# Load order, early layer norms on GpSimd, and matrix squarings held by an identity factor in the setup stage of a two-layer kernel

## The reference

```python
# layer 0
h = layernorm(x) * (1 + ca) + sa                 # sa, ca, ga, ... = silu(c) @ wmod
p = h @ proj_w + proj_b                          # three parts of 128 columns
v = p[0]
for stage in range(2):                           # a convolution with 256 taps through a 512-point FFT
    v = irfft(rfft(v) * rfft(filter[stage])) * p[stage + 1]
x = x + ga * v
x = x + gb * (feed_forward(h) + product_key_experts(h))
# layer 1
x = x + ga * differential_attention(h)           # 16 heads, causal
moe = mixture_of_8_experts(h)                    # w1, gelu, w2, top 2
for i in range(3):
    moe = moe @ expm(gens[i])                    # three 128 x 128 rotations
x = x + gb * gated_mix(abel(h), moe)
```

## Time and profile before

| what | value |
|---|---|
| median of 3 runs | 1199.24 us |
| time of the profiled execution | 1201.76 us |
| span of its profile | 1200.5 us |
| granted TensorE clock, mean | 0.981 |
| busy: TensorE / weight load / VectorE / ScalarE / GpSimd | 1099.8 / 798.7 / 951.9 / 676.3 / 446.5 us |
| first and last transfer of the bulk load | issued at 0.72 us, traffic ends near 34.5 us |
| stage 2 begins (first L1220) | 161.03 us |

### The profile page before, as it was taken

One profiled execution on the slowest core, in us unless ns is written; L12 is line 12 of the kernel. 1 busy time (PEld: TensorE's weight loads), 2 busy tenths in 40 slices (PEclk: granted clock), 3 DMA queues, 4 the chain that ended last, 5 costly groups with the idle time before them and its releaser, 6 DMA issues.

```text
span 1200.5 us, 23140 instructions
## 1 busy us (share of the span) xinstructions
PE 1099.8 (92%) x7614; PEld 798.7 (67%) x7614; DVE 951.9 (79%) x3327; ACT 676.3 (56%) x1739; POOL 446.5 (37%) x724
## 2 busy tenths in 40 slices
PE   0876768999999899999999999999999999999997
PEld 0775734666666676777777677777767777656766
DVE  2496969899998769878888888888888888755767
ACT  0220124555555656776777777767777777744441
POOL 0416413123332315544444444444444555423310
PEclk9998979999999999999999999999999999999999
DMA  9100030000000000000000000000000000000000
GB/s 274 49 1 1 1 106 1 1 1 2 1 1 2 1 1 1 1 1 2 1 1 1 2 2 1 1 1 2 2 1 1 2 1 2 2 1 5 8 9 16
DMA packets 19956, 15.32 MB, mean 13 GB/s; under 512 B 2432, under 2 KB 18816, under 8 KB 19712
## 3 DMA queue, kind: packets, MB, share of 16 engines
q1 hardware_dynamic: 19840, 13.86, 3.9%
HBM read 12.81 MB, written 1.05 MB: 12 GB/s over the span
## 4 chain that ended last, share of the span: by engine, by line
PE 71%; DVE 16%; ACT 5%; issue 4%; POOL 3%; DMA 1%; SPq 1%; DVEq 0%; POOLq 0%; ACTq 0%
PE bank L1549 11%; PE bank L1579 10%; PE bank L1543 10%; PE bank L1498 7%; PE bank L986 5%; PE bank L1887 5%; PE bank L1908 4%; PE bank L1519 3%; PE bank L1527 3%; PE bank L971 2%; ACT prb L1614 2%; DVE prob L1304 2%; DVE xm_e L729 1%; PE bank L964 1%; PE bank L946 1%
## 5 line engine op out<-in xcount | busy, mean ns | idle before, releaser
L1645 POOL TENSOR_SCALAR prb<-prb,rnorm 128x512 f32<-128x512 f32 (+3 forms) x512 | 270.6, 545 | 348.1 <-DVE rnorm L1735 348.0
L1614 ACT ACTIVATE prb<-prb,negmax 128x512 f32<-128x512 f32 (+3 forms) x512 | 281.0, 552 | 113.4 <-DVE negmax L1717 113.4
L1717 DVE CUSTOM_DVE_ANT_0 prb<-bank,mask 128x512 f32<-128x512 f32 (+3 forms) x512 | 218.8, 483 | 18.5 <-PE bank L1543 18.3
L1549 PE MATMUL bank<-ident,prb 128*128 128x128 f32 x1280 | 158.4, 275 | 3.6 <-POOL prb L1645 3.1
L1549 PEld LDWEIGHTS bank<-ident,prb 128*128 128x128 f32 x1280 | 139.6, 141 | 23.3 <-issue 11.6
L1579 PE MATMUL bank<-prbT,vv 128*64 128x512 f32 (+3 forms) x1024 | 151.9, 439 | 0.0
L1579 PEld LDWEIGHTS bank<-prbT,vv 128*64 128x64 f32 x1024 | 63.4, 136 | 82.0 <-issue 81.9
L1622 ACT ACTIVATE prbT<-bank 128x512 f32<-128x512 f32 x128 | 76.5, 597 | 61.2 <-PE bank L1549 60.3
L1726 DVE COPY prbT<-bank 128x512 f32<-128x512 f32 x128 | 87.7, 690 | 14.8 <-PE bank L1549 14.4
L1614 ACT ACTIVATION_READ_ACCUMULATOR prb<-prb,negmax 128x1 f32 x512 | 97.0, 189 | 0.0
L1945 ACT ACTIVATE h<-bank,eb1T 128x512 f32<-128x512 f32 x64 | 43.7, 686 | 55.4 <-PE bank L1887 55.1
(11 more groups left out here) (450 smaller groups left out, 2397.5 us busy)
## 6 DMA issues: line engine op xcount, KB each, us to landing
x<-in_x SPq DMA_DIRECT2D x2, 512.0 KB, 5.9
ew2T<-in_ew2T SPq DMA_DIRECT2D x1, 1024.0 KB, 8.3
ew<-in_ew SPq DMA_DIRECT2D x1, 1024.0 KB, 5.8
wq<-in_Wq SPq DMA_DIRECT2D x2, 512.0 KB, 5.1
wk<-in_Wk SPq DMA_DIRECT2D x2, 512.0 KB, 7.4
wv<-in_Wv SPq DMA_DIRECT2D x1, 1024.0 KB, 8.1
out<-res SPq DMA_DIRECT2D x16, 64.0 KB, 1.5
wmod<-in_wmod SPq DMA_DIRECT2D x2, 384.0 KB, 5.9
```

Source lines behind the costliest of these rows:

```text
L1549: last = T.transpose(into[:, at + (qc - kc) * P:at + (qc - kc + 1) * P], prb[j % 2][:, i, p_at[qc] + kc * P:p_at[qc] + (kc + 1) * P], iden ...
L1614: A.activation(v, v, ACT.Exp, scale=-1.0, bias=negmax[j % 2][:, place[qc], i:i + 1], accum_out=rowsum[j % 2][:, place[qc], i:i + 1]).then_ ...
L1645: last = G.tensor_scalar(v, v, rnorm[j % 2][:, place[qc], i:i + 1], 1.0, ALU.mult, ALU.mult)
L1717: V.tensor_tensor_reduce(prb[j % 2][:, i, p_at[qc]:p_at[qc] + (qc + 1) * P], s_of(j, s, i, qc), mask[:, (NT - 1 - qc) * P:S], 1.0, LARGEST ...
```

## The change

The transfer of `x` for batches 0 and 1 is issued first and `cT`, `small`, `ident` behind it. `c_inv` goes ahead of `gens2` (`xm_b`), and `eb2T` moves behind `ew2T`. GpSimd no longer takes part in the rotations: the maximum over the columns comes from a TensorE transpose, a VectorE maximum and a TensorE broadcast product, and L646 is gone. A finished matrix is held another way: its side 1 is set to the identity, so that the next product leaves side 0 as it is. ScalarE copies side 0 (128x384) and prepares the diagonals keep*I; VectorE does only side 1 (three of 128x128). The rotations begin five rounds in, and the first squaring stands at round 17. The layer norms of batches 2 and 3 get places of their own for `xhat`, `mv` and `rstd` and are done in `setup_*` at round 10, so the second batches' convolutions take 25 rounds. VectorE's first modulation moves behind both first statistics.

```diff
+            SP.dma_start(x[:, 0:2, :, :], tokens[:, 0:2, :, :]).then_inc(x01_in, 16)
             for l in range(2):
                 SP.dma_start(cT[l][:, :], a[f"cT{l}"]).then_inc(first_in, 16)
...
+            SP.dma_start(c_inv[:, :, :], a["c_inv"]...).then_inc(inv_in, 16)
             SP.dma_start(xb, a["gens2"]...).then_inc(rot_in, 16)
-            SP.dma_start(eb2T[:, :], a["eb2T"]).then_inc(rot_in, 16)
...
+            yield from idle(OFFSET)
+            modulation_vector(0)
+            yield from idle(3 + 2 * ORDER + 1 - OFFSET)
             modulation_vector(1)
+            yield from idle(2)
+            V.wait_ge(x23_in, 16)
+            for k in range(2):
+                layernorm_vector(lanes[k], 1, x[:, 2 + k, :, :])
...
+        def rotations_scalar():
+            yield from idle(START + 12)
+            A.wait_ge(xm_ready, 5)
+            for k in range(MAX_SQUARINGS):
+                if k:
+                    A.wait_ge(xm_ps, 4 + k)
+                    A.activation(xe[:, :, 0, :], product(0), ACT.Copy).then_inc(xm_act, 1)
+                if k + 1 < MAX_SQUARINGS:
+                    for i in range(NROT):
+                        last = A.activation(diagonal(k + 1, i), ident[:, :], ACT.Identity, scale=keep[:, k + 1, i:i + 1])
+                    last.then_inc(xm_act, 1)
...
+            yield from idle(START + 1)            # rotations_tensor, START = 5
+            T.wait_ge(xm_norm, 1)
+            T.transpose(bank[0][0:NROT, 0:P], norm[:, :], ident[:, :]).then_inc(xm_all, 1)
+            yield
+            T.wait_ge(xm_norm, 2)
+            T.matmul(bank[0][:, P:P + NROT], largest[:, :].broadcast_to([NROT, P]), ident[0:NROT, 0:NROT], ...)
...
-            G.partition_all_reduce(normall[:, :], norm[:, :], P, MAX_REDUCE).then_inc(xm_all, 1)
-                G.tensor_tensor(kept[k % 2]..., xe..., keep[:, k, :]..., ALU.mult).then_inc(xm_old, 1)
...
+            for i in range(NROT):                 # before the first squaring
+                dve.did(V.tensor_scalar(xe[:, i, 1, :], xe[:, i, 1, :], over[:, 0, i:i + 1], None, ALU.mult))
+            dve.settle()
+            for i in range(NROT):
+                last = V.scalar_tensor_tensor(xe[:, i, 1, :], ident[:, :], keep[:, 0, i:i + 1], xe[:, i, 1, :], ALU.mult, ALU.add)
...
-                    last = V.scalar_tensor_tensor(xe[:, i, :, :], product(i), over[:, k, i:i + 1], old[:, i, :, :], ALU.mult, ALU.add)
+                V.wait_ge(xm_act, DIAGONAL_KEPT(k))
+                    last = V.scalar_tensor_tensor(xe[:, i, 1, :], product(1)[:, i, :], over[:, k, i:i + 1], diagonal(k, i), ALU.mult, ALU.add)
```

More of the change, by code:

```diff
@@ L15 @@
 AX = mybir.AxisListType
-MAX_REDUCE = bass.bass_isa.ReduceOp.max
 P = 128
@@ L424, in sync_program @@
             SP.wait_ge(stored, 16 * NT * B)
+        OFFSET = 2
         def modulation_tensor(l):
@@ L594, in products @@
                     for side in range(2):
-                        last = T.matmul(product(i)[:, side, :], left[:, i, 1 - side, :], right[:, i, side, :],
+                        last = T.matmul(product(side)[:, i, :], left[:, i, 1 - side, :], right[:, i, side, :],
                                         start=True, stop=True)
                 last.then_inc(xm_ps, 1)
-            yield from idle(4)
-            T.wait_ge(rot_in, ROT_IN)
+            yield from idle(START + 1)
+            T.wait_ge(xm_norm, 1)
+            T.transpose(bank[0][0:NROT, 0:P], norm[:, :], ident[:, :]).then_inc(xm_all, 1)
+            yield
+            T.wait_ge(xm_norm, 2)
+            T.matmul(bank[0][:, P:P + NROT], largest[:, :].broadcast_to([NROT, P]), ident[0:NROT, 0:NROT], start=True, stop=True).then_inc(xm_all, 1)
+            yield
+            yield
             products(xb, xb, 1)
@@ L637, in rotations_tensor @@
             yield
-        def rotations_gpsimd():
-            G.wait_ge(xm_norm, 1)
-            G.partition_all_reduce(normall[:, :], norm[:, :], P, MAX_REDUCE).then_inc(xm_all, 1)
[L642 to L650, removed]
         def rotations_vector():
-            V.wait_ge(rot_in, ROT_IN)
+            yield from idle(START)
+            V.wait_ge(rot_in, 16)
             V.tensor_reduce(norm[:, :], xb[:, :, 0, :], AX.X, ALU.add, apply_absolute_value=True).then_inc(xm_norm, 1)
@@ L676, in rotations_vector, with coefficients, constant @@
             yield
[L677 to L689, removed]
+            def coefficients(dst, c0, c1, c2):
+                V.wait_ge(xm_ready, 2)
                 dve.did(V.tensor_scalar(flat(dst), flat(xb), c1, None, ALU.mult))
-                yield
                 dve.settle()
                 dve.did(V.scalar_tensor_tensor(flat(dst), flat(xb2), c2, flat(dst), ALU.mult, ALU.add))
-                yield
+            def constant(dst, c0):
                 dve.settle()
@@ L699, in poly @@
                 return last
-            last = yield from poly(xp, *TAYLOR[6:9])
+            yield
+            V.wait_ge(xm_ps, 1)
+            for side in range(2):
+                last = V.tensor_copy(xb2[:, :, side, :], product(side))
             last.then_inc(xm_ready, 1)
             yield
-            last = yield from poly(xe, *TAYLOR[3:6])
-            dve.did(last)
+            coefficients(xp, *TAYLOR[6:9])
             yield
+            V.wait_ge(xm_ps, 2)
+            for side in range(2):
+                dve.did(V.tensor_copy(xb3[:, :, side, :], product(side)))
@@ L707, in rotations_vector @@
+            constant(xp, TAYLOR[6]).then_inc(xm_ready, 1)
+            V.wait_ge(xm_ready, 3)
+            yield
+            coefficients(xe, *TAYLOR[3:6])
+            yield
+            dve.did(constant(xe, TAYLOR[3]))
+            V.wait_ge(xm_ps, 3)
             dve.settle()
-            V.wait_ge(xm_ps, 3)
-            for i in range(NROT):
-                last = V.tensor_tensor(xe[:, i, :, :], xe[:, i, :, :], product(i), ALU.add)
+            for side in range(2):
+                last = V.tensor_tensor(xe[:, :, side, :], xe[:, :, side, :], product(side), ALU.add)
@@ L711, in rotations_vector @@
             last.then_inc(xm_ready, 1)
             yield
-            last = yield from poly(xp, *TAYLOR[0:3])
-            dve.did(last)
+            coefficients(xp, *TAYLOR[0:3])
             yield
+            dve.did(constant(xp, TAYLOR[0]))
+            V.wait_ge(xm_ps, 4)
             dve.settle()
-            V.wait_ge(xm_ps, 4)
+            for side in range(2):
+                dve.did(V.tensor_tensor(xe[:, :, side, :], xp[:, :, side, :], product(side), ALU.add))
+            dve.settle()
@@ L787, in convolutions_tensor @@
         def convolutions_tensor(w, n0, b):
-            yield from idle(2)
+            if n0 == 0:
+                yield from idle(2)
             yield from transposed_tensor(w, n0)
```

113 lines of the change are left out of this document (69 added, 44 removed).

## The result

The changed kernel takes 1161.68 us, the median of 4 runs (1161.15 to 1164.17), beside 1198.57 (1197.53 to 1200.09) for the kernel before. The ratio is 0.9695, with a 95% interval of 0.9677 to 0.9714. The forecast was 1163.

A forecast was written before the change was run, and what follows sets the result against it. It took transfers, then TensorE, to bound the start and VectorE the squarings (61.85 of 72.9 us). Gains of 17.8 + 18.9 + 0 = 36.7 us took 1199.24 to 1162.5, stated as 1163, range 1154 to 1178.

The forecast's parts named there:

- The start: Up to the first filter product: it moves from 35.05 to 13.8 us, 21.2 us earlier.
- From the filter to the first squaring: Stretch from 13.8 to 59 us: first squaring 17.8 us earlier, 3.4 of the 21.2 won given back.
- The list: VectorE's operations before the first squaring, from 25 us on: 31.3 us of work plus 2.7 of waits on TensorE.
- The squarings: First squaring to final products: 72.9 us becomes 54, bounds 49 and 62, a gain of 18.9, with TensorE the bound.
- the lock: In the squarings, VectorE operations held until GpSimd's L646 ends: 12.0 us of VectorE time that leaves.
- The half width: In the squarings, VectorE combines only half: 20.2 us becomes 13.4, a gain of 6.8.
- Rival (b): The squarings lose only the lock and the batch-2 gap: 61 us there, 1170 in all; chance 0.08.
- (d): In the squarings TensorE runs at 1.2 GHz, its 47.7 us becoming 95.4: 1211 us in all; chance 0.02.
- The tail: The final products up to stage 2, 11.3 us: no change, 0 with bounds -1 and +1.
- The sum: Whole kernel: 17.8 + 18.9 + 0 = 36.7 us less, giving 1163.
- the early `x`: At the start, `x` issued at 0.72 us lands at 4.5, so `xhat` is complete at 10.4.

The follow-up runs named there:

- the maximum alone: The kernel before with only the column maximum moved from GpSimd's all-reduce to TensorE and VectorE: 1186.04 us, beside 1200.78 for the kernel before.
- the old form: The changed kernel with the old squarings (GpSimd multiplies 128x768, VectorE combines three of 128x256, no ScalarE): 1176.67 us.
- the lock by itself: The changed kernel with 15 unread two-input GpSimd multiplications of 128x768 added, one behind each combination: 1170.12 us.
- the added work: GpSimd operations of 128x768 that nobody reads, added to the changed kernel: 1170.12 us with two inputs, 1164.96 us with one.
- the early feed-forward norm: The changed kernel with the feed-forward's first layer norm (batch 0) moved to round 30 of the setup: 1154.75 us, and 1154.65 in a second group.

## Why the prediction was right

**The start.** Forecast 21.2 us, measured 35.05 - 13.12 = 21.9. The removed pause was the cause, as the maximum alone showed. One step was off and hidden: I took the small loads to land with `x`. They landed at about 7.8, so `xhat` was complete at 12.1 and not at 10.4, and the transposes ended just as `c_filt` landed. Had `xhat` come any later, the filter product would have moved with it.

**From the filter to the first squaring.** Forecast 45.2 us (13.8 to 59), measured 44.2. The list was forecast from 25 on, with 31.3 us of work and 2.7 of waits. The transposed norm was out at 23.7, and from there to 57.3 VectorE is busy 30.9 of 33.6 us; TensorE waits 5.7 us for it before the first squaring. That is 2.4 us more than before, in the direction that I gave (3.4).

**The squarings.** Forecast 54, measured 54.2. The bound did pass from VectorE to TensorE, and the prices held: three combinations take 0.87 (0.89 forecast), copy and diagonals 0.49 + 0.97 = 1.46 (1.4), a cycle with a convolution block 3.13 (3.13). The closeness of the sum is luck in part, for two errors cancel. I said that TensorE's work doesn't change, 47.7 us, and it is busy for 52.1. The first squaring moved from round 19 to round 17 but the first batches of the lanes did not move with it, so 12 convolution blocks fall behind it and not 11, one more of 1.79 us; and the first squaring (2.93 us instead of 1.50) and the block behind it (2.52 instead of 1.95) ran at a granted clock of 0.62 (57.3 to 62.4 us), after the 5.7 us that TensorE had stood; from 62.4 on it is 1.00.

Against that, TensorE is idle for 2.1 us only, where 54 left it 6.3. VectorE's 45.4 beside my 40.2 has the same source: 6 `fold` pairs instead of 5, 6 of the last multiplication with `pv` (L934) instead of 4, and two of `mpair` now lie in this stretch.

The runs take the gain apart like this: the old form costs 16.0 us of stretch, and the lock by itself holds VectorE for 11.3 us (12.0 forecast), of which 7.7 reach the stretch while the rest falls into VectorE's new slack. The half width was measured only together with the lock. Rival (b) is out with 54.2 beside 61, and (d) too, at a granted clock of 0.96: TensorE fell to half rate in the first 5 us alone. `xhat` of batch 2 was complete 33 us ahead of its transposes, not 50, which was still enough.

**The tail.** Forecast 0; measured 121.7 - 111.5 = 10.2 beside 11.3, so 1.1 better, just outside the bound of 1. The cause was not looked for; the granted clock there was 0.83 beside 0.70.

**The sum.** 36.7 forecast. The medians differ by 36.9, the two profiled spans by 39.8. By points of the two profiles the gain is 19.5 to the first squaring (17.8 forecast), 18.7 in the squarings (18.9) and 1.1 in the tail (0), 39.3 in all, 2.6 more than the forecast. That the medians miss it by 0.2 only is therefore luck in part: the profiled execution of before lies 3.2 above its median, as in the forecast it lay 2.5 above, and that of the changed kernel 0.3.

The load order was the part for which I had no term of its own but the early `x`. Undone singly it costs 1.5 us by the medians, and the ranges overlap.

## What to carry to other kernels

A call that pauses an engine costs what is queued behind it: read whose instruction follows it, before replacing it with other engines' work, since placing it behind the urgent work was here worth as much. Once the bound of a stretch is known, follow the rounds with the trace's own durations, and count the blocks anew when one stream moves against the others: the forecast had TensorE's work at 47.7 us, it was 52.1, and only a generous allowance for waits brought the sum to within 1%. And after a gain, look for the same kind of gap at the next passage: a statistics chain whose input had been ready for 48 us was worth 7 us more.

## What the runs showed of the hardware that wasn't expected

- The pause after the all-reduce need not stand directly behind it: in one kernel a CAST ran at once, and 7.87 us of pause stood before the TENSOR_SCALAR that followed; in the kernel before, the TENSOR_SCALAR came directly, behind 10.52 us. Whether the kind of operation decides this or its place behind the call was not tried.
- A one-input GpSimd operation of 128x768 holds a two-input VectorE operation as a two-input one does. Held operations of 128x256 end 0.26 to 0.28 us after GpSimd's, held ones of 128x512 some 0.55 us (142.60 beside 142.05 in the earlier trace rows). VectorE's operations with an input in PSUM kept their time beside the added work: the combination took 0.339 us on average, 0.343 without it.
- It goes the other way too: `xhat` of batch 2 took 4.51 us on GpSimd where VectorE worked beside it, and one of the first `xhat` took 3.12 where VectorE stood idle. L920 beside the former took 0.84 instead of 0.69.
- With nothing changed, the first squaring stood at 57.13 and at 60.12 us in two executions of one kernel (the early feed-forward norm). The same block of products in both:

```profile
28.56 2.05 PE L879 MATMUL bank<-fold,c_fwd_sb 128*128 128x128 f32 x16 [1.38 <-DVE fold L936]
29.58 3.78 PE L879 MATMUL bank<-fold,c_fwd_sb 128*128 128x128 f32 x16 [1.38 <-DVE fold L936]
```

TensorE had waited for the same 1.38 us before it in both. In the first execution the granted clock was 1.00 from 28 to 36 us, in the second 0.62 from 28 to 37. They had parted before that: the first filter product, at the low rate at its start in both, took 4.27 us in the first and 5.38 in the second. So behind the same short wait the clock may or may not be down, from one execution to the next, and here that moved the first squaring by some 3 us. What decides it is not shown.
